# Count-matrix stage of a graph kernel: wider register loads, two groups emptied at a time, two waits per round

## The reference

```python
def _L0_gnn_ref(x, edge_index, num_steps):
    row, col = (edge_index[0], edge_index[1])
    for _ in range(num_steps):
        w = _gcn_norm(row, col, n_nodes, x.dtype)   # dinv[row] * dinv[col]
        msgs = w[:, None] * x[row]
        x = jax.ops.segment_sum(msgs, col, num_segments=n_nodes)
    return x
...
x = _layernorm(x + _L0_gnn_ref(x, edge_index, 4), axis=-1)
x = _layernorm(x + _L1_gnn_ref(...), axis=-1)
x = _layernorm(x + _L2_gnn_ref(...), axis=-1)
x = _layernorm(x + _L3_gnn_ref(...), axis=-1)
```

## Time and profile before

| | before |
|---|---|
| time, median of 3 runs | 5742.42 us (5738.28 to 5754.01) |
| profiled execution, its own time | 5746.0 us |
| its span | 5744.3 us |
| TensorE clock granted, mean of the span | 0.632 |
| matrix-building stage, from its first instructions to the barrier behind it | about 274 to 740 us of the span |

### The profile page before, as it was taken

One profiled execution on the slowest core, in us unless ns is written; L12 is line 12 of the kernel. 1 busy time (PEld: TensorE's weight loads), 2 busy tenths in 40 slices (PEclk: granted clock), 3 DMA queues, 4 the chain that ended last, 5 costly groups with the idle time before them and its releaser, 6 DMA issues. The chain is left out here.

```text
span 5744.3 us, 76417 instructions
## 1 busy us (share of the span) xinstructions
PE 2918.6 (51%) x18212; PEld 2315.4 (40%) x18213; DVE 3740.9 (65%) x6525; ACT 1779.5 (31%) x5291; POOL 3421.0 (60%) x3372
## 2 busy tenths in 40 slices
PE   4344578724555554363745335546463345554642
PEld 1233456514544444242433234445453234444542
DVE  4645554217777777133243578999997579998987
ACT  0055500001111111100010046565655146555563
POOL 4077237737777776441722477777770677777760
PEclk7655589956666666575867655556565555656655
DMA  6131040036777776400000222212120221222211
GB/s 213 34 101 52 0 141 2 2 90 198 217 217 218 220 217 188 167 9 3 1 7 9 56 49 50 53 46 53 46 46 20 51 54 45 53 49 49 53 31 17
DMA packets 491937, 449.21 MB, mean 78 GB/s; under 512 B 135358, under 2 KB 439156, under 8 KB 491651
## 3 DMA queue, kind: packets, MB, share of 16 engines
q1 hardware_dynamic: 257947, 232.05, 14.3%
q0 software_dynamic: 116768, 136.51, 10.0%
q10 hardware_dynamic: 116936, 77.08, 4.2%
HBM read 308.22 MB, written 137.16 MB: 78 GB/s over the span
## 5 line engine op out<-in xcount | busy, mean ns | idle before, releaser
L2104 POOL DMA_INDIRECT tg<-tab_d,tail_ids x1632 | 1706.0, 1045 | 565.4 <-issue 494.6
L445 POOL DMA_INDIRECT sorted_edges_d<-place_batch x784 | 806.0, 1028 | 747.5 <-DMA place_batch<-place_queue_d 340.1
L2137 PE MATMUL acc<-msg,sum_hot 128*96 128x65 f32 x3264 | 547.0, 366 | 984.9 <-ACT msg L2206 781.8
L2137 PEld LDWEIGHTS acc<-msg,sum_hot 128*96 128x96 f32 x3264 | 529.4, 279 | 1001.0 <-issue 1001.0
L1494 POOL DMA_INDIRECT xg<-tab_d,src_i x784 | 769.3, 981 | 252.3 <-issue 238.5
L2127 PE MATMUL hr<-near_table,near_hot 128*128 x4896 | 679.8, 268 | 196.6 <-DVE near_hot L2253 94.3
L2127 PEld LDWEIGHTS hr<-near_table,near_hot 128*128 128x128 f16 x4896 | 496.5, 105 | 381.1 <-issue 282.7
L2181 ACT ACTIVATE pr<-hr 128x396 f32<-128x396 f32 x576 | 277.1, 482 | 592.3 <-PE hr L2127 590.7
L2195 ACT ACTIVATE msg<-tg,coef_b 128x64 f32<-128x64 f32 x1632 | 396.7, 334 | 31.2 <-DVEq L2596 31.2
L1508 PE MATMUL hq<-ex,sameU 128*128 128x128 f32 x1568 | 273.8, 354 | 258.3 <-DVEq L1613 192.1
L2201 ACT ACTIVATE pr<-pr,coef_c 128x64 f32<-128x64 f32 x1632 | 398.6, 334 | 0.0
(11 more groups left out here) (461 smaller groups left out, 5368.7 us busy)
## 6 DMA issues: line engine op xcount, KB each, us to landing
ex<-spread_d SPq DMA_DIRECT2D x112, 448.0 KB
msg_d<-back ACTq DMA_DIRECT2D x112, 448.0 KB
near_hot<-head_row_d SPq DMA_DIRECT2D x96, 408.0 KB
tg<-tab_d,tail_ids POOLq DMA_INDIRECT x1632, 2.5
spread_d<-zeros ACTq DMA_DIRECT2D x28, 896.0 KB, 10.9
spread_d<-zeros SPq DMA_DIRECT2D x28, 896.0 KB, 8.7
idsU<-dst_short_d SPq DMA_DIRECT2D x112, 224.0 KB
pairs_d<-pair_m SPq DMA_DIRECT2D x3, 4800.0 KB
```

Source lines behind the costliest of these rows:

```text
L445: l.eng.indirect_dma_start(K.sorted_edges[:, :], bass.IndirectOffsetOnAxis(ap=K.batch[:, n % 2, 0, k:k + 1], axis=0), K.batch[:, n % 2, 1, ...
L2104: e.indirect_dma_start(tg[:, u % TAILS * GQ + k, :], None, K.tab3, bass.IndirectOffsetOnAxis(ap=K.tail_ids[:, u * GQ + k:u * GQ + k + 1], ...
L2137: ins = e.matmul(sums[:, bass.ds(at[k], D + 1)], sum_hot[u % 2][:, k, :], msg[u % QN][:, k, :], start=False, stop=False, skip_group_check= ...
```

## The change

1. `K.step_regs` gets two counts a round in place of one: the count for step 4 (`half`) and the count for step 8 (`whole`); a round has 10 words, all used. One more small VectorE instruction makes it.
2. TensorE loads the values of both rounds of a turn with one load at the head of the turn: 20 values instead of twice nine. In a round it checks `half` and waits for it before step 1, and checks `whole` and waits for it before step 5.
3. ScalarE empties two neighbouring groups with one pair of instructions, on 2x200 columns, after the second of them is complete, and adds 2 to `emptied`. `K.group_ends` holds only the counts of the second groups. The last group, the 391st, is emptied alone.
4. ScalarE loads the 12 counts of 24 groups with one load at the head of a turn, instead of eight counts three times.

```diff
-            v.tensor_scalar(K.step_regs[:, :, SG:SG + 1], at_i[:, :].rearrange("o (r k) -> o r k", k=SG)[:, :, SG - 1:SG], 1.0, None, ALU.add).then_inc(l.sem, l.add(1))
+            for n in range(2):
+                v.tensor_scalar(K.step_regs[:, :, SG + n], at_i[:, :].rearrange("o (r k) -> o r k", k=SG)[:, :, SG // 2 * (n + 1) - 1], 1.0, None, ALU.add).then_inc(l.sem, l.add(1))
...
+            seconds = lambda x: x[:, 0:GROUPS - 1].rearrange("o (g two) -> o g two", two=2)[:, :, 1]
             v.wait_ge(spread, 5)
-            v.scalar_tensor_tensor(K.group_ends[:, :], ps[0][0:1, 3, 0:GROUPS + 1], float(AHEAD), count[0:1, 0:GROUPS + 1], ALU.add, ALU.add).then_inc(l.sem, l.add(1))
+            v.scalar_tensor_tensor(K.group_ends[:, :], seconds(ps[0][0:1, 3, :]), float(AHEAD), seconds(count[0:1, :]), ALU.add, ALU.add).then_inc(l.sem, l.add(1))
...
             with l.loop(ROUNDS // 2) as i:
-                for s in range(2):
-                    *regs, least = load_values(nc, mybir.EngineType.PE, K.step_regs[0:1, bass.ds(i * 2 + s, 1), 0:SG + 1].rearrange("p o k -> p (o k)"),
-                                               0, (SG - 1) * 512)
-                    least = nc.s_assert_within(least, 1, GROUPS)
-                    e.wait_ge(emptied, least)
+                at = load_values(nc, mybir.EngineType.PE, K.step_regs[0:1, bass.ds(i * 2, 2), :].rearrange("p o k -> p (o k)"), 0, (SG - 1) * 512)
+                for r in range(2):
+                    *regs, half, whole = at[r * (SG + 2):(r + 1) * (SG + 2)]
+                    e.wait_ge(emptied, nc.s_assert_within(half, 1, GROUPS))
                     e.sem_inc(l.sink, 1)
-                    e.wait_ge(made, i * 4 + (s + 1) * 2)
+                    e.wait_ge(made, i * 4 + (r + 1) * 2)
                     e.sem_inc(l.sink, 1)
                     for k in range(SG):
-                        e.matmul(banks[:, bass.ds(regs[k], KW)], lows[s][:, :, k], cells[s][:, k, :],
+                        if k == SG // 2:
+                            e.wait_ge(emptied, nc.s_assert_within(whole, 1, GROUPS))
+                            e.sem_inc(l.sink, 1)
+                        e.matmul(banks[:, bass.ds(regs[k], KW)], lows[r][:, :, k], cells[r][:, k, :],
                                  start=False, stop=False, skip_group_check=True).then_inc(stepped, 1)
...
-            def empty(bank, column):
-                sums = ring[:, bank, 0:KW]
-                a.activation(m[:, :, column], sums.rearrange("p (h d) -> p h d", d=GD), ACT.Copy, scale=0.5).then_inc(l.sem, l.add(1))
+            def empty(bank, two, column):
+                sums = ring[:, bank:bank + two, 0:KW]
+                a.activation(m[:, :, column].rearrange("p h (g d) -> p g h d", d=GD), sums.rearrange("p g (h d) -> p g h d", d=GD), ACT.Copy, scale=0.5).then_inc(l.sem, l.add(1))
                 a.wait_ge(l.sem, l.done())
-                a.activation(sums, sums, ACT.Copy, scale=0.0).then_inc(emptied, 1)
+                a.activation(sums, sums, ACT.Copy, scale=0.0).then_inc(emptied, two)
             turn = 3 * SG
             with l.loop(GROUPS // turn) as i:
-                for c in range(0, turn, SG):
-                    over = load_counts(nc, mybir.EngineType.Activation, K.group_ends[0:1, bass.ds(i * turn + c, SG)], NS + AHEAD)
-                    for b in range(SG):
-                        a.wait_ge(stepped, over[b])
-                        empty(b, bass.ds(i * (turn * GD) + (c + b) * GD, GD))
+                over = load_counts(nc, mybir.EngineType.Activation, K.group_ends[0:1, bass.ds(i * (turn // 2), turn // 2)], NS + AHEAD)
+                for n in range(turn // 2):
+                    a.wait_ge(stepped, over[n])
+                    empty(2 * n % SG, 2, bass.ds(i * (turn * GD) + 2 * n * GD, 2 * GD))
```

More of the change, by code:

```diff
@@ L645, in step_views @@
 def step_views(K, room):
-    keys, regs = ROUNDS * 3 * SG // 2, ROUNDS * (SG + 4)
+    keys, regs = ROUNDS * 3 * SG // 2, ROUNDS * (SG + 2)
     K.step_keys = room[:, 0:keys].bitcast(F16).rearrange("p (r k) -> p r k", k=3 * SG)
-    K.step_regs = room[0:1, keys:keys + regs].bitcast(I32).rearrange("p (r k) -> p r k", k=SG + 4)
-    K.group_ends = room[0:1, keys + regs:keys + regs + GROUPS + 1].bitcast(I32)
+    K.step_regs = room[0:1, keys:keys + regs].bitcast(I32).rearrange("p (r k) -> p r k", k=SG + 2)
+    K.group_ends = room[0:1, keys + regs:keys + regs + GROUPS // 2].bitcast(I32)
 def build_pairs(nc, K, m):
@@ new lines, in scalar @@
+                for n in range(turn // 2):
+                    a.wait_ge(stepped, over[n])
+                    empty(2 * n % SG, 2, bass.ds(i * (turn * GD) + 2 * n * GD, 2 * GD))
+            left = GROUPS // turn * turn
+            assert GROUPS - left < SG and GROUPS % 2 == 1
+            over = load_counts(nc, mybir.EngineType.Activation, K.group_ends[0:1, left // 2:GROUPS // 2], NS + AHEAD)
+            for n in range((GROUPS - left) // 2):
+                a.wait_ge(stepped, over[n])
+                empty(2 * n, 2, slice((left + 2 * n) * GD, (left + 2 * n + 2) * GD))
@@ L744, in scalar @@
+            a.wait_ge(stepped, NS + AHEAD)
+            empty(GROUPS % SG - 1, 1, slice((GROUPS - 1) * GD, GROUPS * GD))
             a.wait_ge(emptied, GROUPS + SG)
```

## The result

| | before | after |
|---|---|---|
| median | 5751.5 us (8 runs, 5738.28 to 5754.01) | 5766.65 us (8 runs, 5761.03 to 5775.79) |
| ratio after / before | | 1.0035, 95% interval 1.0026 to 1.0045 |
| profiled execution, span | 5744.3 us | 5769.5 us |
| matrix stage, first product of the stage to first instruction behind its barrier | 465.7 us | 486.8 us |
| a turn of TensorE's loop, median of the stage | 5.90 us | 6.24 us |

The change made the kernel slower by a third of a per cent, some 20 us by the ratio (the two medians lie 15.2 us apart, the means 19.2). The span of the profiled executions grew by 25.2 us. Of this 21.1 us lie in the matrix stage; 1.5 us lie ahead of it and 2.5 us behind it, no more than these parts differ between kernels that leave them alone (the part behind the stage is 5003.8 to 5019.7 us in the traces of this study).

A forecast was written before the change was run, and what follows sets the result against it. The prediction took TensorE's sequencer, its instructions carried out one after the other, as the bound. Per turn -1.07 + 0.70 + 0.65 + 0.26 = +0.54 us, over 74 turns +40 us: 5742.4 + 40 = 5782 us, range 5763 to 5812.

The forecast's parts named there:

- The bound: Matrix stage: TensorE's sequencer is occupied all the time, its instructions and gaps making the 5.90 us turn.
- Removed: 1.07 us a turn: TensorE's sequencer: the second load and its address instruction, with their gaps, go once a turn, saving 1.07 us.
- Added: a wider load, +0.70 us: TensorE's sequencer: one load of 20 values in place of nine takes 1.54 us, +0.70 a turn, bounds +0.50 to +1.04.
- Added: two checks and two waits, 0.91 us: TensorE's sequencer: two more checks a turn cost 0.65 us and two more waits 0.26 us.
- Not hidden in mid-round: TensorE's round: the new check and wait count in full, though they stand while products are queued.
- Slow loads, no change: TensorE's loads during the zero stores: 27 us lost may become some 20 to 45; taken as 27, no change.
- ScalarE at zero: Matrix stage: TensorE's waits for ScalarE's emptying cost zero, despite ScalarE's longer stop at the head of its turn.
- The margin of +0.6 us: ScalarE's turn head: about +0.6 us left before TensorE needs the bank, 9.8 - 6.6 - 1.35 - 1.2.
- The late ScalarE: Rival: ScalarE makes TensorE wait one to two us in each of its 16 turns, 5798 to 5814 us; 12 in 100.
- The almost fixed cost: Rival: TensorE's wide load costs little more than the narrow one, about 5738 to 5752 us; 7 in 100.
- The 0.17 us a value: Rival: each further value in TensorE's load costs 0.17 us, as in slow loads, stage +127 us, 5869; 4 in 100.
- The faster case: Rival: TensorE's mid-round checks and waits are hidden under queued products, -0.37 us a turn, -27 us, 5715; 4 in 100.

The follow-up runs named there:

- the wide load alone: Kernel before, with TensorE loading a turn's 20 values at once, still one count a round, ScalarE as before: ratio 0.9945, turn 5.37 us.
- the two counts alone: Kernel before, with two counts checked and waited for each round, two loads a turn: ratio 1.0366 with rows of 10 words, 5848.98 us with 12.
- the 19 loads above: Kernel with 20-value load and one count a round, plus 19 loads of varied width and first word behind TensorE's loop: 12 aligned values 0.852 us.

## Why the prediction was right, and where its sizes were off

- **The bound.** That a turn is the sum of the sequencer's instructions, whoever the waits view names, held in every kernel in which ScalarE was in time: parts that were costed as instructions moved the turn by -0.53 (wide load), +0.85 (second count) and -0.38 us (maximum).
- **The size, and luck.** The ratio is 1.0035 where I forecast 1.007: half the change. The time, 5766.65 us, lies 16 us below the forecast of 5782 and only 4 us above the low end of my range. It lies inside because of luck: the median of before, on which I built, came out 9.1 us higher over eight runs (5751.5) than over three (5742.42). From 5742.42 the measured ratio gives 5762.5, just outside. Also, 5764 to 5808, which I gave as the forecast's own bounds, don't follow from my terms; 5782 with -15 - 7 and with +25 + 18 is 5760 to 5825.
- **Removed: 1.07 us a turn.** Right; the wide load alone gives 1.07 - 0.51 = 0.56 for a measured 0.53.
- **Added: a wider load, +0.70 us.** This is the step that was mis-sized. I drew a line in the number of values through the earlier trace rows. The load behaves as if it read 16 bytes at a time: nine values are three reads, 17 and 20 are both five. It cost +0.51 us; 74 x 0.19 = 14 us of the forecast's 40. My lower bound, the 17-value row itself, was the true value.
- **Added: two checks and two waits, 0.91 us.** Measured 0.85 with the loads taken out, 4 us less over the stage, and 0.87 between the kernel after and the same with one count a round. In a regular turn of the trace after, a check in mid-round takes 0.286 us to the wait behind it, where I had 0.323 with the mean gaps, and the wait 0.151, where I had 0.128. The step itself was right.
- **Not hidden in mid-round.** Right: the products' spread from 1.55 to 1.79 us shows the second count inside the round.
- **Slow loads, no change.** Their time above the median load fell from 26.8 to 22.6 us, a gain of 4 us inside the 20 to 45 I allowed. Two readings behind that term were wrong. The 3.47 us of the earlier trace rows are the idle time before the round at 417.94; it is late by 1.85 us, for it comes 5.03 us after the one at 412.91 instead of 3.18. And the 4.236 us of the earlier trace rows aren't a slowed load, so my 3.2 us for a slow load of 20 values had no ground; that most of them are slower by just 3.2 us (4.5 to 4.6 us in the trace after, the longest 4.92) is luck. The stage's account closes: 74 x 0.343 = 25.4, less 4.2, is 21.2 us of the measured 21.1.
- **ScalarE at zero.** True for the change: no second round is late. The margin of +0.6 us rested on TensorE asking in half rounds and on its longer turn; without the second count, which gives both, six second rounds came late.
- **Rivals.** The late ScalarE didn't happen here but did with one count a round. The almost fixed cost was half right in kind, as 17 and 20 values cost the same, but not for nine against 20. The 0.17 us a value was false: the 4.2 us of the earlier trace rows that it leaned on are the price of a first value off the 16 bytes, not of transfers. The faster case is excluded by the two counts alone.

The forecast's own terms hold a gain (-1.07 + 0.70 = -0.37 us a turn) and a loss (+0.91), but it looked at their sum alone. Taken apart, the wide load brings 39 us of turns and the second count costs 63.

## What to carry to other kernels

Where rounds follow one another at exactly equal distances and no engine is busy, list the sequencer's instructions of one turn with their times: loads into registers, checks and waits are then the work, and the releasers named by the waits view are not. Cost each part of a change by itself, since one can pay for another. A load into registers should begin on a multiple of 16 bytes and be filled up to one (nine values cost what twelve do, 0.86 and 0.85 us, and the same nine 2.18 us one word further on); a check of a value is dearer than the wait that it guards; and a helper engine that stops long at its turn's head sets how far ahead its results may be asked for.

## What the runs showed of the hardware

- A load of words from on-chip memory into TensorE's registers takes as long as if it cost 0.08 us and 0.255 us for each read, a read fetching four values if the first lies on a multiple of 16 bytes (4 values 0.337 us, 12 0.852, 20 1.357), and values left over being read one by one (10 values 1.096). If the first is off, each value costs as a read of its own: 2.177 us for nine, 4.732 for 20. The rule was on record before the 19 loads above were measured. The Trainium skill ("Runtime: NRT & Kernel Launch", instruction fetch mechanics) puts the load of a register from HBM at about 200 ns. The loads here are from on-chip memory: those off the boundary come near that figure, at 0.237 us a value, and those on it don't, at 0.068.
- While the large stores of zeros run, most such loads are slower by some 0.64 us for each read: 1.9 us for nine values (2.7 to 2.9 in place of 0.847), 3.2 for 20 (4.5 to 4.6 in place of 1.360). With the stores out of the stage the longest load of 20 values took 1.56 us.
- A check of a register against two bounds takes TensorE's sequencer 151 + 18 ns and two gaps, 0.286 us in all; a maximum takes 34 ns and one gap. The turn with two of the one in place of two of the other was 0.38 us shorter.
- ScalarE reloaded its table for 1.28 us at the head of each of its 16 turns, though one function is used throughout; it is part of the stop behind which late rounds come.
